# Attention stage on eight cores: the row-sum matmuls spread between the score and attention-times-V matmuls, and a fourth scratch buffer

## The chip, the cores and the metric

The kernel runs on the 8 cores of one Trainium2 chip. Each core takes one of the 8 batch items (x[c], 2048 tokens by 2048 features) with all the weights and writes its own part of the output; the cores exchange nothing. The metric is the device time of the slowest core in microseconds (us).

## The reference, cut to what matters

One transformer layer: layer norm, attention with 16 query heads and 4 key/value heads (head size 128), a feed-forward part, and the product of both on top of x.

```python
xn = _layernorm(x)
s = attn(xn)                      # below
g = silu(ffn(xn))                 # 2048 -> 5632 -> 2048
out = x + s * g
# attn, per head h, S = 2048:
q, k = rope(rms_norm(xn @ Wq.T)), rope(rms_norm(xn @ Wk.T)); v = xn @ Wv.T
bias = einsum('bhsr,bhtr->bhst', Rq, Rk)   # rank 32, heads 0..11; heads 0..3 made symmetric
scores = einsum('bhsd,bhtd->bhst', q, k) * scale + bias
attn = softmax(where(causal, scores, min), axis=-1)
out = einsum('bhst,bhtd->bhsd', attn, v) @ Wo.T
```

## The kernel before, in words

The program is a row of stages: p0 (layer norm and transposes), p1 (v, k and the rank-32 projections), p2 (q), p3 (feed-forward in two halves of the tokens), p4 (attention), p5 (the Wo projection), p6 (gating and output). The engines run their own instruction streams and meet at semaphores; within an engine the order is the order of the code. The change touches p4 alone.

p4 works in four blocks g = 0 to 3 (called blocks 1 to 4 here), each over 512 query tokens (a barrier stands between blocks). In block g each of the 16 heads h goes over nch = 4g + 4 chunks of 128 keys. Scores are kept with keys on the partitions and the 512 queries along the row.

- TensorE (from L1123). For chunk j: the score matmul (L1155, p_sc<-p_qg,p_kfm), for heads 0 to 11 a bias matmul (L1162) into the same bank, for heads 0 to 3 a second one (L1168). So a chunk costs three, two or one score matmuls in heads 0 to 3, 4 to 11 and 12 to 15. The score bank sc_ps has room for two pairs of chunks: a pair waits (eEv) until VectorE has emptied the pair two before it. From chunk 6 on, after the scores of chunk j comes the attention-times-V matmul ("AV") of chunk j - 6 (L1179), and after the loop the last six AVs (L1186). Each waits (eEx) for the exponentials of its pair. Then come the nch row-sum matmuls (L1194, p_sm<-p_ptb,c_onesc: a column of ones times the exponentials, into one row sm_ps), after a wait (eSv) for sm_ps to be empty; the last one signals eAV. Then bcast (L1134) of head h - 1: a matmul that copies the reciprocal of its sums to all partitions (rb_ps). Before a head from h = 2 on starts, TensorE waits (eNo) until VectorE has finished tail(h - 2).
- VectorE. For head h: sums_evac(h - 1) (L1208, empties sm_ps, signals eSv), then each pair of chunks from sc_ps to the scratch scr, as one copy of 128x1024 (L1241) or, in the last four chunks, as two additions of the causal mask (L1253, 128x512); then tail(h - 1): rb_ps to rb_sb (L1218) and the normalised output to ogs (L1222), which waits (eB2) for bcast(h - 1). Here sums_evac and tail of a head come one head late. A pair takes scratch buffer pr % 3, and waits (eEx) until ScalarE has read what was in it.
- ScalarE. Per pair the exponential of the scratch into ptb (L1290, bf16), with a bound found before as the bias; after a head's pairs recip_chain(h - 1) (L1275 and L1278: logarithm, then exponential of the negative), which signals eSm, for which bcast waits.
- SyncE loads the q of 8 heads at a time (L1105, L1114; the second load waits for head 7's last sum matmul) and stores ogs.

```python
if h >= 1:
    tensor.wait_ge(eSv.h, base_eSv + h)
for jj in range(nch):
    mm2 = tensor.matmul(sm_ps[0:1, 0:512], onesc[:, :], ptb[:, jj * 512:(jj + 1) * 512],
                        start=(jj == 0), stop=(jj == nch - 1))
mm2.then_inc(eAV.h, 1)
if h >= 1:
    bcast(tensor, h - 1)
```

Of the kernel before, what the change touches and what calls it, by code (L numbers as in the profile page):

```python
# [9 lines left out]
F32 = mybir.dt.float32  # L10
# [37 lines left out]
def build_program(taps=(), stop_after=None):  # L48
# [53 lines left out]
    with ExitStack() as L0:  # L102
# [5 lines left out]
        onesc = sbuf("c_onesc", [128, 1], BF16)  # L108
# [47 lines left out]
        with ExitStack() as SA:  # L156
# [5 lines left out]
            with ExitStack() as SP:  # L162
                sb = lambda n, sh, dt: SP.enter_context(nc.sbuf_tensor(n, sh, dt))
# [775 lines left out]
        if go("p4"):  # L939
            with ExitStack() as SP:  # L940
# [146 lines left out]
                eQl = sem("eQl"); eSp4 = [sem(f"eSp{i}") for i in range(4)]  # L1087
                scr = sb("p4_scr", [128, 3 * 1024], F32)
                for g in range(NG):
                    nch = 4 * g + 4  # L1090
                    with nc.Block(f"p4g{g}") as block:
# [39 lines left out]
                        def _(tensor):  # L1131
# [10 lines left out]
                            for h in range(NH):  # L1142
# [7 lines left out]
                                for j in range(nch):  # L1150
# [25 lines left out]
                                    if j >= 6:  # L1176
# [5 lines left out]
                                            ptb[:, jj * 512:(jj + 1) * 512],  # L1182
                                            start=(jj == 0), stop=False)
                                for jj in range(max(0, nch - 6), nch):
                                    tensor.wait_ge(eEx.h, base_eEx + pbase + jj // 2 + 1)
# [4 lines left out]
                                        start=(jj == 0), stop=(jj == nch - 1))  # L1190
                                if h >= 1:
                                    tensor.wait_ge(eSv.h, base_eSv + h)
                                for jj in range(nch):
                                    mm2 = tensor.matmul(  # L1194
                                        sm_ps[0:1, 0:512],
                                        onesc[:, :], ptb[:, jj * 512:(jj + 1) * 512],
                                        start=(jj == 0), stop=(jj == nch - 1))
                                mm2.then_inc(eAV.h, 1)
# [6 lines left out]
                        def _(vector):  # L1205
# [24 lines left out]
                            for h in range(NH):  # L1230
                                if h >= 1:
                                    sums_evac(vector, h - 1)
                                for j in range(0, nch, 2):
                                    pr = ich // 2
                                    if pr >= 3:
                                        vector.wait_ge(eEx.h, base_eEx + pr - 2)
                                    po = (pr % 2) * 1024
                                    so = (pr % 3) * 1024
                                    if j + 1 < 4 * g:
# [29 lines left out]
                        def _(scalar):  # L1269
# [14 lines left out]
                            for h in range(NH):  # L1284
                                for p in range(nch // 2):
# [5 lines left out]
                                        ptb[:, j0 * 512:(j0 + 2) * 512],  # L1291
                                        scr[:, (pr % 3) * 1024:(pr % 3) * 1024 + 1024],
                                        AF.Exp,
# [248 lines left out]
```

## Time and profile before

| what | value |
|---|---|
| time, median of 3 runs | 4578.66 us (lowest 4578.41) |
| profiled execution: its own time | 4576.78 us |
| its span on core 7, the slowest | 4575.2 us (the eight cores: 4552.0 to 4575.2) |
| mean granted TensorE clock of the core | 0.901 of full speed |
| TensorE matmul busy | 3566.5 us, 78% of the span |
| VectorE, ScalarE busy | 1117.7 us (24%), 906.3 us (20%) |
| p4, four blocks | 3108.6 to 4166.6 us of the span |

The profile is of one execution on the slowest core. A table of stretches gives the busy time of each engine in a window, with the number of instructions, and the clock that TensorE was granted, as a share of full speed (2.4 GHz; the other level is 1.2 GHz). The timeline lists instructions with their start, duration, engine, line, output and inputs; "xN" stands for N alike in a row, and what is in brackets is how long the engine sat idle before it and what ended that. A matmul of 512 columns is listed with 0.38 us from its start to its end at the full clock, but the next one can start earlier; the distance between starts is what it costs in a stream.

### The profile page before, as it was taken

The page shows a single profiled execution, that of the slowest core. Times are in us where ns is not written, and L with a number is a line of the kernel's source. Part 1 is how long each engine was busy: PE and PEld are TensorE (multiplying, and loading weights), DVE is VectorE, ACT ScalarE, POOL GpSimd, SP SyncE. Part 2 cuts the span into 40 slices and gives each one's busy share as a digit, 9 for nine tenths or more (in the row PEclk, how much of TensorE's full clock was granted, in tenths as well). Part 3 has the DMA queues.
Part 4 walks back from the last instruction along what each step waited for, and adds up shares of the span by engine and source line. Part 5 has one row for each costly group of instructions (what it writes and reads, how often), then busy time and mean ns, then how long its engine had stood idle before and what let it go on. Part 6 is the DMA issues. An engine that isn't in the chain of part 4 may idle for free. (4 is left out here: it accounts for less than half of the span.)

```text
span 4575.2 us, 38843 instructions; the slowest of 8 cores (4552.0 to 4575.2 us)
## 1 busy us (share of the span) xinstructions
PE 3566.5 (78%) x15274; PEld 1498.9 (33%) x15274; DVE 1117.7 (24%) x1179; ACT 906.3 (20%) x895; POOL 390.9 (9%) x343
## 2 busy tenths in 40 slices
PE   2576477776999998998999999764677877785973
PEld 1222122222444443443444444321122222222433
DVE  7132133342001000000000000023444554552006
ACT  2121033331000000001000000002333444452112
POOL 0000011111111110001111110000000000000000
PEclk9977788888999999999999999987787988997986
DMA  3311412214777864547777855441000000003347
GB/s 130 62 12 19 109 30 37 35 30 51 79 74 75 80 67 73 75 74 82 76 74 78 79 60 78 78 115 45 20 19 19 7 18 15 15 6 92 38 115 276
DMA packets 547235, 287.85 MB, mean 63 GB/s; under 512 B 457075, under 2 KB 528756, under 8 KB 540020
## 3 DMA queue, kind: packets, MB, share of 16 engines
q0 software_dynamic: 498480, 162.55, 33.2%
q1 hardware_dynamic: 48580, 122.82, 7.8%
q8 instruction: 128, 2.10, 0.2%
q14 instruction: 47, 0.39, 0.0%
HBM read 397.53 MB, written 50.33 MB: 98 GB/s over the span
## 5 line engine op out<-in xcount | busy, mean ns | idle before, releaser
L900 PE MATMUL p_dps<-p_hfm,p_dwb 128*128 128x512 bf16 x2816 | 625.6, 385 | 86.2 <-ACT p_gout L918 59.6
L828 PE MATMUL p_gps<-xn_fm,p_gwb 128*128 128x512 bf16 x2816 | 626.6, 381 | 39.1 <-DMA p_uwb<-wu 39.1
L835 PE MATMUL p_ups<-xn_fm,p_uwb 128*128 128x512 bf16 x2816 | 622.1, 379 | 0.0
L861 DVE SCALAR_TENSOR_TENSOR p_hfm<-p_ups,c_ups,p_sg 128x1024 bf16<-128x1024 f32 x88 | 113.0, 1284 | 1499.8 <-ACT p_sg L850 1499.8
L1290 ACT ACTIVATE p_ptb<-p_scr,st_bnegb 128x1024 bf16<-128x1024 f32 x320 | 366.2, 1148 | 524.5 <-DVE p_scr L1241 408.9
L1155 PE MATMUL p_sc<-p_qg,p_kfm 128*128 128x512 bf16 x640 | 280.9, 456 | 193.1 <-DVE p_ogs L1222 97.6
L900 PEld LDWEIGHTS p_dps<-p_hfm,p_dwb 128*128 128x128 bf16 x2816 | 277.4, 99 | 434.3 <-issue 116.5
L828 PEld LDWEIGHTS p_gps<-xn_fm,p_gwb 128*128 128x128 bf16 x2816 | 276.5, 98 | 375.6 <-issue 46.5
L835 PEld LDWEIGHTS p_ups<-xn_fm,p_uwb 128*128 128x128 bf16 x2816 | 275.5, 98 | 332.3
L697 PE MATMUL p_qps<-xn_fm,p_wbuf 128*128 128x512 bf16 x1024 | 287.0, 438 | 37.6 <-DMA p_wbuf<-wq 37.6
L850 ACT ACTIVATE p_sg<-p_gps,c_gates 128x1024 f32<-128x1024 f32 x88 | 98.1, 1115 | 1089.7 <-PE p_ups L835 1089.6
L1241 DVE COPY p_scr<-p_sc 128x1024 f32<-128x1024 f32 x192 | 232.3, 1223 | 135.6 <-PE p_sc L1162 61.8
L1342 PE MATMUL p_sps<-p_osb,p_wob 128*128 128x512 bf16 x1024 | 223.9, 382 | 39.4 <-DMA p_wob<-wo 39.4
L1162 PE MATMUL p_sc<-p_rqs,p_rku 128*128 128x512 bf16 x480 | 208.8, 435 | 0.0
L1155 PEld LDWEIGHTS p_sc<-p_qg,p_kfm 128*128 128x128 bf16 x640 | 67.0, 108 | 385.1 <-issue 355.1
L810 POOL DMA_DIRECT2D p_gwb<-wg x88 | 100.7, 1144 | 1016.6 <-PE p_ups L835 990.2
L697 PEld LDWEIGHTS p_qps<-xn_fm,p_wbuf 128*128 128x128 bf16 x1024 | 106.5, 109 | 221.0 <-issue 141.2
L1186 PE MATMUL p_o<-p_ptb,p_vsb 128*128 128x512 bf16 x352 | 110.5, 402 | 79.5 <-ACT p_ptb L1290 78.9
L1253 DVE TENSOR_TENSOR p_scr<-p_sc,p_masks 128x512 f32<-128x512 f32 x256 | 163.3, 684 | 32.6 <-PE p_sc L1168 18.3
L1342 PEld LDWEIGHTS p_sps<-p_osb,p_wob 128*128 128x128 bf16 x1024 | 100.8, 99 | 163.6 <-issue 44.5
L1194 PE MATMUL p_sm<-p_ptb,c_onesc 128*1 128x512 bf16 x640 | 153.5, 388 | 0.0
L918 ACT ACTIVATE p_gout<-p_dps,c_downs 128x1024 bf16<-128x1024 f32 x32 | 34.1, 1111 | 512.6 <-PE p_dps L900 478.8
(138 smaller groups left out, 2486.4 us busy)
## 6 DMA issues: line engine op xcount, KB each, us to landing
p_gwb<-wg POOLq DMA_DIRECT2D x88, 512.0 KB, 6.3
p_uwb<-wu POOLq DMA_DIRECT2D x88, 512.0 KB, 8.1
p_dwb<-wd POOLq DMA_DIRECT2D x88, 512.0 KB, 5.7
p_xt<-x SPq DMA_DIRECT2D x32, 1024.0 KB, 8.1
y<-p_outb SPq DMA_DIRECT2D x16, 1024.0 KB, 11.0
p_wbuf<-wq POOLq DMA_DIRECT2D x16, 512.0 KB, 6.4
sp_q<-p_qout SPq DMA_DIRECT2D x64, 128.0 KB, 1.8
sp_g<-p_gout SPq DMA_DIRECT2D x32, 256.0 KB, 3.0
```

The costliest lines, as they stand in the source:

```text
L697: mm = tensor.matmul(qps[:, po + q4 * 512:po + (q4 + 1) * 512], wv_[:, ec * 128:(ec + 1) * 128], xn_cols(ec, hh * 1024 + q4 * 512, 512), s ...
L828: tensor.matmul(gps[:, po + q4 * 512:po + (q4 + 1) * 512], gw_[:, ec * 128:(ec + 1) * 128], xn_cols(ec, hh * 1024 + q4 * 512, 512), start= ...
L835: mm = tensor.matmul(ups[:, po + q4 * 512:po + (q4 + 1) * 512], uw_[:, ec * 128:(ec + 1) * 128], xn_cols(ec, hh * 1024 + q4 * 512, 512), s ...
L861: vector.scalar_tensor_tensor(hfm[:, ic * 1024:(ic + 1) * 1024], ups[:, po:po + 1024], ups_c[:, ic:ic + 1], sg[:, po:po + 1024], ALU.mult, ...
L900: mm = tensor.matmul(dps[:, oc4 * 1024 + q4 * 512: oc4 * 1024 + (q4 + 1) * 512], wv_[:, oc4 * 128:(oc4 + 1) * 128], hfm[:, ic * 1024 + q4 ...
L1155: last = tensor.matmul(sc_ps[:, po:po + 512], kfm[:, kv * S + j * 128: kv * S + (j + 1) * 128], qg[:, (h % 8) * 512:(h % 8 + 1) * 512], st ...
L1162: last = tensor.matmul(sc_ps[:, po:po + 512], rku[:, h * S + j * 128: h * S + (j + 1) * 128], rqs[:, oc * S + g * 512: oc * S + (g + 1) * ...
L1194: mm2 = tensor.matmul(sm_ps[0:1, 0:512], onesc[:, :], ptb[:, jj * 512:(jj + 1) * 512], start=(jj == 0), stop=(jj == nch - 1))
L1241: vector.tensor_copy(scr[:, so:so + 1024], sc_ps[:, po:po + 1024]).then_inc(eEv.h, 1)
L1253: op = vector.tensor_tensor(scr[:, soc:soc + 512], sc_ps[:, poc:poc + 512], masks[:, k * 512:(k + 1) * 512], ALU.add)
L1290: scalar.activation(ptb[:, j0 * 512:(j0 + 2) * 512], scr[:, (pr % 3) * 1024:(pr % 3) * 1024 + 1024], AF.Exp, bias=bneg_b[:, col:col + 1]). ...
L1342: mm = tensor.matmul(sps[:, po + q4 * 512:po + (q4 + 1) * 512], wv_[:, ec * 128:(ec + 1) * 128], osb[:, ec * S + q4 * 512: ec * S + (q4 + ...
```

## The change

The nch sum matmuls of a head are issued in groups of four, each behind the AV of the last chunk of its group (jj % 4 == 3), wherever that AV stands: in the loop over the chunks (new line 1188) or after it (new line 1203). The wait for eSv moves to the first group. The accumulation in sm_ps now lies between matmuls into o_ps and sc_ps, which are other banks. The scratch scr has four buffers of 1024 columns in place of three, and VectorE's wait for a free one goes back one pair further. No instruction of VectorE, ScalarE or SyncE moves.

```diff
-                scr = sb("p4_scr", [128, 3 * 1024], F32)
+                scr = sb("p4_scr", [128, 4 * 1024], F32)
...
                                             start=(jj == 0), stop=False)
+                                        if jj % 4 == 3:
+                                            if jj == 3 and h >= 1:
+                                                tensor.wait_ge(eSv.h, base_eSv + h)
+                                            for js in range(jj - 3, jj + 1):
+                                                tensor.matmul(
+                                                    sm_ps[0:1, 0:512], onesc[:, :],
+                                                    ptb[:, js * 512:(js + 1) * 512],
+                                                    start=(js == 0), stop=False)
                                 for jj in range(max(0, nch - 6), nch):
                                     tensor.wait_ge(eEx.h, base_eEx + pbase + jj // 2 + 1)
...
-                                if h >= 1:
-                                    tensor.wait_ge(eSv.h, base_eSv + h)
-                                for jj in range(nch):
-                                    mm2 = tensor.matmul(
-                                        sm_ps[0:1, 0:512],
-                                        onesc[:, :], ptb[:, jj * 512:(jj + 1) * 512],
-                                        start=(jj == 0), stop=(jj == nch - 1))
+                                    if jj % 4 == 3:
+                                        if jj == 3 and h >= 1:
+                                            tensor.wait_ge(eSv.h, base_eSv + h)
+                                        for js in range(jj - 3, jj + 1):
+                                            mm2 = tensor.matmul(
+                                                sm_ps[0:1, 0:512], onesc[:, :],
+                                                ptb[:, js * 512:(js + 1) * 512],
+                                                start=(js == 0), stop=(js == nch - 1))
...
-                                    if pr >= 3:
-                                        vector.wait_ge(eEx.h, base_eEx + pr - 2)
+                                    if pr >= 4:
+                                        vector.wait_ge(eEx.h, base_eEx + pr - 3)
                                     po = (pr % 2) * 1024
-                                    so = (pr % 3) * 1024
+                                    so = (pr % 4) * 1024
...
-                                        scr[:, (pr % 3) * 1024:(pr % 3) * 1024 + 1024],
+                                        scr[:, (pr % 4) * 1024:(pr % 4) * 1024 + 1024],
```

On TensorE, the end of a head with two score matmuls a chunk in block 4 (16 chunks), before. p_sc are scores, p_o is AV, p_sm are the sums, p_rb is the broadcast:

```order
L1155 MATMUL p_sc<-p_qg,p_kfm 128x512
L1162 MATMUL p_sc<-p_rqs,p_rku 128x512
L1179 MATMUL p_o<-p_ptb,p_vsb 128x512
L1186 MATMUL p_o<-p_ptb,p_vsb 128x512 x6
L1194 MATMUL p_sm<-p_ptb,c_onesc 1x512 x16
L1134 MATMUL p_rb<-p_recip,c_onesr 128x512
```

The same place after the change, from the AV of chunk 7 on:

```order
L1179 MATMUL p_o<-p_ptb,p_vsb 128x512
L1188 MATMUL p_sm<-p_ptb,c_onesc 1x512 x4
L1155 MATMUL p_sc<-p_qg,p_kfm 128x512
L1162 MATMUL p_sc<-p_rqs,p_rku 128x512
L1179 MATMUL p_o<-p_ptb,p_vsb 128x512
L1155 MATMUL p_sc<-p_qg,p_kfm 128x512
L1162 MATMUL p_sc<-p_rqs,p_rku 128x512
L1179 MATMUL p_o<-p_ptb,p_vsb 128x512
L1194 MATMUL p_o<-p_ptb,p_vsb 128x512 x2
L1203 MATMUL p_sm<-p_ptb,c_onesc 1x512 x4
L1194 MATMUL p_o<-p_ptb,p_vsb 128x512 x4
L1203 MATMUL p_sm<-p_ptb,c_onesc 1x512 x4
L1134 MATMUL p_rb<-p_recip,c_onesr 128x512
```

Of the 16 sums that stood together ahead of the broadcast, four are left there; four stand between the AVs after the loop, and eight in the loop (four of them shown, four more behind AV 3). In block 2 (8 chunks), TensorE at the end of such a head, before:

```order
L1155 MATMUL p_sc<-p_qg,p_kfm 128x512
L1162 MATMUL p_sc<-p_rqs,p_rku 128x512
L1179 MATMUL p_o<-p_ptb,p_vsb 128x512
L1186 MATMUL p_o<-p_ptb,p_vsb 128x512 x6
L1194 MATMUL p_sm<-p_ptb,c_onesc 1x512 x8
L1134 MATMUL p_rb<-p_recip,c_onesr 128x512
```

And after:

```order
L1155 MATMUL p_sc<-p_qg,p_kfm 128x512
L1162 MATMUL p_sc<-p_rqs,p_rku 128x512
L1179 MATMUL p_o<-p_ptb,p_vsb 128x512
L1194 MATMUL p_o<-p_ptb,p_vsb 128x512 x2
L1203 MATMUL p_sm<-p_ptb,c_onesc 1x512 x4
L1194 MATMUL p_o<-p_ptb,p_vsb 128x512 x4
L1203 MATMUL p_sm<-p_ptb,c_onesc 1x512 x4
L1134 MATMUL p_rb<-p_recip,c_onesr 128x512
```

Here no sum stands ahead of a score matmul of the same head.

## Rows read from the trace of the kernel before

**Rows 1.** Stretches, p4's blocks: us, busy PE PEld DVE ACT POOL, PEclk, DMA.

```profile
3108.60:3289.80 181.20, 108.68 (x288) 30.87 (x288) 74.05 (x112) 56.37 (x65) 0.00 (x0) 0.75 0.07 24
3289.80:3521.80 232.00, 163.81 (x544) 52.99 (x544) 108.93 (x144) 93.00 (x97) 0.00 (x0) 0.84 0.06 19
3521.80:3813.40 291.60, 217.39 (x800) 75.58 (x800) 148.12 (x176) 129.57 (x129) 0.00 (x0) 0.89 0.05 15
3813.40:4166.60 353.20, 278.38 (x1056) 99.26 (x1056) 186.81 (x208) 166.25 (x161) 0.00 (x0) 0.90 0.04 13
```

**Rows 2.** Waits in 3100 to 4170: us in total, times, longest.

```profile
PE p_sc L1155 <- DVE p_ogs L1222: 97.6, 52, 2.2
PE p_o L1186 <- ACT p_ptb L1290: 78.9, 117, 2.1
...
PE p_sc L1155 <- DVE p_scr L1241: 23.5, 50, 1.0
...
DVE p_scr L1241 <- ACT p_ptb L1290: 1.3, 1, 1.3
```

**Rows 3.** Timeline, TensorE, end of head 11 in block 4.

```profile
4067.92 0.38 PE L1179 MATMUL p_o<-p_ptb,p_vsb 128*128 128x512 bf16 x1
4068.26 0.38 PE L1155 MATMUL p_sc<-p_qg,p_kfm 128*128 128x512 bf16 x1
...
4069.12 0.38 PE L1162 MATMUL p_sc<-p_rqs,p_rku 128*128 128x512 bf16 x1
...
4069.55 0.59 PE L1186 MATMUL p_o<-p_ptb,p_vsb 128*128 128x512 bf16 x2
4070.70 0.59 PE L1186 MATMUL p_o<-p_ptb,p_vsb 128*128 128x512 bf16 x2 [0.55 <-ACT p_ptb L1290]
4071.89 0.59 PE L1186 MATMUL p_o<-p_ptb,p_vsb 128*128 128x512 bf16 x2 [0.60 <-ACT p_ptb L1290]
4072.42 3.61 PE L1194 MATMUL p_sm<-p_ptb,c_onesc 128*1 128x512 bf16 x16
4075.96 1.12 PE L1134 MATMUL p_rb<-p_recip,c_onesr 1*128 1x512 f32 x2
4079.00 1.86 PE L1155 MATMUL p_sc<-p_qg,p_kfm 128*128 128x512 bf16 x4 [1.92 <-DVE p_ogs L1222]
```

**Rows 4.** Timeline, ScalarE, the same head.

```profile
4068.21 3.54 ACT L1290 ACTIVATE p_ptb<-p_scr,st_bnegb 128x1024 bf16<-128x1024 f32 x3 [0.27 <-DVE p_scr L1241]
...
4072.34 0.63 ACT L1278 ACTIVATE p_recip<-p_recip 1x512 f32<-1x512 f32 x1
```

**Rows 5.** Timeline, TensorE, end of head 0 in block 4 (last score matmul, last AVs).

```profile
3833.21 0.38 PE L1168 MATMUL p_sc<-p_rksh,p_rqu 128*128 128x512 bf16 x1
...
3835.77 0.59 PE L1186 MATMUL p_o<-p_ptb,p_vsb 128*128 128x512 bf16 x2 [1.11 <-ACT p_ptb L1290]
```

**Rows 6.** Timeline, TensorE, end of head 13 in block 4.

```profile
4107.61 0.38 PE L1179 MATMUL p_o<-p_ptb,p_vsb 128*128 128x512 bf16 x1
4108.10 0.38 PE L1155 MATMUL p_sc<-p_qg,p_kfm 128*128 128x512 bf16 x1
...
4108.53 0.38 PE L1155 MATMUL p_sc<-p_qg,p_kfm 128*128 128x512 bf16 x1
...
4111.73 0.59 PE L1186 MATMUL p_o<-p_ptb,p_vsb 128*128 128x512 bf16 x2 [0.60 <-ACT p_ptb L1290]
```

**Rows 7.** Timeline, TensorE, last AVs of head 15 in block 2.

```profile
3508.79 0.59 PE L1186 MATMUL p_o<-p_ptb,p_vsb 128*128 128x512 bf16 x2 [0.33 <-ACT p_ptb L1290]
```

**Rows 8.** Timeline, TensorE, end of head 6 in block 1.

```profile
3179.15 1.02 PE L1194 MATMUL p_sm<-p_ptb,c_onesc 128*1 128x512 bf16 x4
3180.10 1.12 PE L1134 MATMUL p_rb<-p_recip,c_onesr 1*128 1x512 f32 x2
```

**Rows 9.** Stretches: behind a head's end in block 4, and 40 us of the feed-forward stage.

```profile
4119.40:4125.40 6.00, 5.26 (x13) 1.51 (x12) 4.80 (x4) 3.68 (x4) 0.00 (x0) 0.50 0.07 24
...
2420.00:2460.00 40.00, 40.00 (x187) 18.18 (x186) 3.85 (x3) 3.35 (x3) 6.85 (x6) 1.00 0.74 73
```

## The prediction

> **What bounds the kernel now.** I read the table of stretches first, one row for each of the four query blocks of the attention stage [rows 1]. The stage is 1058 us of 4575.2, and TensorE is the busiest engine in every block: in the last 278.4 us of 353.2, against 186.8 for VectorE and 166.2 for ScalarE. So the stage ends when TensorE has done its matmuls, and what can be won without taking matmuls away is TensorE's idle time (72.5, 68.2, 74.2 and 74.8 us in the four blocks) and the time in which its clock is low. The waits say what the idle time is made of [rows 2]: 97.6 us before the first score matmul of a head, until VectorE has normalised the head before the last (p_ogs); 78.9 us before an attention-times-V matmul ("AV" below), until ScalarE's exponentials (p_ptb) are there; 23.5 us before a score matmul, until VectorE has emptied the score bank. Then I went through one head in order of time.
>
> Rows 3 are the end of a head with two score matmuls per chunk, in the fourth block. Matmuls of one stream start 0.216 us apart. The last score matmul starts at 4069.12, the AV of chunk 9 follows, then AV 10 and 11; AV 12 and 13 wait for ScalarE (0.55 idle), AV 14 and 15 again (0.60). Only then come the 16 row-sum matmuls, 3.61 us, then the broadcast of the previous head's reciprocal at 4075.96, then 1.92 us idle until VectorE is done, and at 4079.00 the next head's scores. During the sums VectorE and ScalarE have nothing to do. What ends this chain is the last exponential, not TensorE's own work: TensorE stands idle twice while it holds matmuls that could run. ScalarE ends the head's exponentials just before 4071.75 (4068.21 + 3.54) and the reciprocal at 4072.97 [rows 4].
>
> **The change, part by part.** It removes no matmul and adds none. (a) The sums of chunks 0 to 3 go behind AV 3, and so on by fours. A block of 4 chunks has the old order. With 8 chunks both groups of sums lie behind the last score matmul: the first moves ahead of AV 4. With 12 chunks one group moves in between score matmuls and one between AV 7 and AV 8. With 16 chunks two groups move in between score matmuls and one between AV 11 and AV 12. Four sums always stay at the end. One group is 4 x 0.216 = 0.86 us. (b) The wait for the emptied sum bank comes earlier in the head. VectorE empties that bank ahead of the head's first score copy, several us before AV 3, so I cost the wait at nothing. (c) VectorE's scratch gets a fourth buffer. VectorE waited 1.3 us in all for a free one [rows 2]: nothing, and at most 1.3.
>
> What (a) gives is TensorE's idle time that the moved sums fill. I take G, the time from the end of the last score matmul's slot to the start of the last AV pair. In G lie five AVs (1.08 us) and idle time. Nothing can make G shorter than VectorE's last masking, the last exponential and the semaphores between them.
>
> Heads 0 to 3 (three score matmuls a chunk): TensorE sets the pace in the loop, so its row shows the shortest G [rows 5]: 3835.77 - 3833.42 = 2.35 us (the slot of the last score matmul, from 3833.21, ends at 3833.42), 1.27 of it idle. One group of sums fits, 0.41 stays idle. A group placed among the score matmuls only delays them, and comes back as shorter work at the end. Gain 0.86 in each of the three blocks: 12 heads x 0.86 = 10.3 us.
>
> Heads 4 to 11 (two score matmuls): G = 4071.89 - 4069.34 = 2.55 us [rows 3], 1.47 idle. The group in G gives 0.86. In blocks 3 and 4 the groups in the loop delay the last score matmul, and G may then shrink to 2.35: another 0.20. They also fill the small holes that TensorE has in the loop: from 4067.92 to 4068.26 is 0.34 instead of 0.216, a hole of 0.13, and there are two such behind the first group in block 4 (0.26), while in block 3 I take 0.05. Block 2: 0.86, block 3: 1.11, block 4: 1.32. Eight heads each: 26.3 us.
>
> Heads 12 to 15 (one score matmul): VectorE sets the pace. G = 4111.73 - 4108.74 = 2.99 us, and the hole from 4107.61 to 4108.10 is 0.27 [rows 6]. Block 4: 0.86 + (2.99 - 2.35) + 2 x 0.27 = 2.04. Block 3: one group in the loop costs 0.86 - 0.27 = 0.59, which G takes up whole, so the whole 1.73 us of two groups would be won; one of its four heads has less idle time, so I take 1.6. Block 2: the gain is the idle before the last AVs; it differs between the four heads, the last one has 0.33 us listed [rows 7], which is some 0.5 between the slots; I take 0.5. Four heads each: 4 x (0.5 + 1.6 + 2.04) = 16.6 us.
>
> Sum: 10.3 + 26.3 + 16.6 = 53 us.
>
> What is late next? After the change the last sum ends 0.86 us after AV 15, about 1.4 us after the last exponential, and the broadcast behind it needs ScalarE's reciprocal, which ends 1.3 us after the exponential [rows 4]. That is close, but block 1 already has just this order, and there the broadcast follows the four sums at once (sums from 3179.15, broadcast at 3180.10, no idle) [rows 8]. So it costs nothing. The wait for p_ogs (1.92) stays as it is, since VectorE's two operations follow the broadcast. The block ends and the two loads of Q in each block stay too.
>
> Bounds of this term. If a group in the loop delays VectorE by its whole length and fills no hole, each head wins only the group in G: 44 x 0.86 + 4 x 0.5 = 40 us. If every moved sum were free, the gain would be (4 + 8 + 12) x 16 x 0.216 = 83 us. I take 53, since rows 3, 5 and 6 are nearest to it.
>
> The unknown is the clock. The granted clock is 0.75, 0.84, 0.89 and 0.90 in the four blocks [rows 1], which is a mixture of the two levels, 1.2 and 2.4 GHz: low for 50%, 32%, 22% and 20% of the time. In blocks 2 to 4 that is 74 + 64 + 71 = 209 us at the low level, of which TensorE is busy about three quarters (659.6 of 876.8 us), and half of that is lost: 78 us. It falls after the idle time at a head's end: the stretch of 6 us behind such an end is at 0.50, and dense work just before this stage was at 1.00 [rows 9]. The change makes the idle time before the last AV shorter and leaves the 1.9 us; it also brings the two nearer to each other. I see no sign for one direction and take nothing, with 20 us either way.
>
> The Trainium skill, TensorE: Matmul & The Clock Gate, section "A second HAM failure mode: psum-queue depth-cycling", says that a kernel whose TensorE idles briefly and often between groups of matmuls sees its clock go to and fro. This trace agrees: 0.84 to 0.90 in blocks with three or four short waits a head, against 1.00 in the dense stretch. By that rule fewer waits mean more clock, which is rival B below.
> The same page, in its section "Seeing it yourself", warns of a limiter that lowers the clock of a die to 13/16 once three of its cores run dense matmuls. That would speak against filling TensorE's holes. This trace does not show it: 1.00 in the dense stretch, with all eight cores at the same work.
>
> The profiled execution took 4576.8 us (span 4575.2), the median of the runs shown is 1.9 us above. So 4576.8 - 53 = 4523.8 by the profile and 4525.6 against the median: I say 4525.
>
> **The rivals.** (A) The sums in the loop delay VectorE fully. For it: VectorE's copies run nearly back to back in the loop, and TensorE is never more than two pairs ahead of it; against it: the holes of 0.13 and 0.27 us. Gain 40, time 4539.
>
> (B) The clock rises as the waits go. If half of the low time in blocks 2 to 4 went away, 39 us more: 4486. For it: the clock is higher the less of a block TensorE idles (0.75 at 40% idle, 0.90 at 21%) [rows 1]; against it: the 1.9 us wait, after which it falls, is left in every head.
>
> (C) The clock falls, and the change is slower than before. Place: the end of a head in blocks 2 to 4. The dense run of 8 to 16 sums ahead of the 1.9 us idle becomes 4 sums, which is the shape of block 1, and block 1 has 0.75. At 0.75 the work of blocks 2 to 4, 877 - 53 - 78 = 746 us, would stretch by the low half: T = 746 + 0.5 x T x 0.75 / 2, T = 918, against 824: 94 us more, 4576.8 - 53 + 94 = 4618. It decides from the point where the loss by the low clock reaches 78 + 53 = 131 us: 349 us at the low level, 40% of the blocks, a mean clock of 0.80. Against it: block 1's heads are 10 us with the same idle time as the heads of 20 us in block 4, so it has twice as much of it per us.
>
> (D) The change does not do what it says: the filled holes come back before the broadcast or at the p_ogs wait, since ScalarE's reciprocal is only 0.1 us ahead. Then 4577. Against it: rows 8.
>
> **How the numbers follow.** Forecast 0.70, A 0.13, B 0.08, C 0.06, D 0.03. Range: at the fast end all moved sums free (4577 + 2 - 83 = 4496), or B in part; at the slow end A with 15 us lost by the clock: 4554. I give 4492 to 4555; B's far end, C and D lie outside. A change of over 2% (92 us, about what a measurement of this kernel can tell from no change) needs a time under 4487 or over 4670. Faster by that much: 0.06, most of B. Slower by that much: 0.02, the far end of C, since C itself is only 0.9% slower. Within 2%: 0.92.
>
> **What would show each step.** Right: TensorE's busy time in the stage and the count of sum matmuls as before; TensorE's wait for p_ptb down from 78.9 us to about 40 (block 1's 27 stay, and some 0.3 a head elsewhere); the wait for p_ogs still near 98 us; VectorE's wait for the broadcast shorter by 0.9, 1.7 and 2.6 us a head in blocks 2, 3 and 4, less what the loop gives back; block 1 unchanged in length, block 2 about 12, block 3 about 19, block 4 about 22 us shorter; in blocks 2 to 4 a granted clock within 0.02 of now. Wrong: a new wait of the broadcast for p_recip in each head (D); VectorE waiting longer for p_sc in the loop and the last exponential late by the whole 0.86 or 1.73 us (A); a mean clock of blocks 2 to 4 above 0.93 (B) or under 0.80 (C).

## The result, and the profile after

The changed kernel takes 4548.6 us in the median of 23 runs, the kernel before 4583.5 us in the same series. The ratio is 0.9921, with a 95% interval of 0.9903 to 0.9939: some 36 us (28 to 44) faster, or 0.8%, where 53 us were forecast. Some executions of every kernel take longer, with a lower granted clock on the cores of one die: the ratios leave them out, and one profile below is therefore read on six cores. "Block lengths" are means over the eight cores of the profiled executions, from one block's first load of Q to the next block's. A mean of eight cores moves by about 1 us between profiles of the same order of work.

| kernel | block 1 | block 2 | block 3 | block 4 | stage | ratio to before (95%) |
|---|---|---|---|---|---|---|
| before | 182.5 | 232.8 | 292.0 | 354.4 | 1061.7 | |
| after | 182.7 | 222.8 | 277.6 | 339.4 | 1022.4 | 0.9921 (0.9903 to 0.9939) |
| forecast for after | as before | -12 | -19 | -22 | -53 | |

The stretches of the four blocks after, on the slowest core, to lay beside [rows 1] (columns as there):

```profile
3107.40:3289.00 181.60, 110.34 (x288) 30.82 (x288) 74.08 (x112) 56.60 (x65) 0.00 (x0) 0.75 0.07 24
3289.00:3513.00 224.00, 170.71 (x544) 52.04 (x544) 109.60 (x144) 93.18 (x97) 0.00 (x0) 0.80 0.06 19
3513.00:3790.30 277.30, 222.79 (x800) 71.44 (x800) 149.65 (x176) 130.12 (x129) 0.00 (x0) 0.88 0.05 16
3790.30:4127.80 337.50, 283.25 (x1056) 93.61 (x1056) 188.48 (x208) 166.94 (x161) 0.00 (x0) 0.89 0.04 13
```

The reader is to see two things. The count of matmuls in each block is the same, and block 1 is unchanged. But TensorE's busy time has grown in blocks 2 to 4: 163.8, 217.4 and 278.4 us before, 170.7, 222.8 and 283.3 now. In means of eight cores the stage went from 771.4 us busy and 290.3 idle to 784.8 busy and 237.7 idle. So 52.7 us of listed idle time went, and 13.4 us came back as longer work for the same matmuls.

That 52.7 is so near the 53 of the forecast is partly luck. A matmul is listed 0.16 us longer than its slot of 0.216, so each wait that goes takes less listed idle time with it than it is worth; and by the account below the changed order fills 9 us of idle time more than the forecast counted. The two work against each other.

The waits of the stage after, beside [rows 2]:

```profile
PE p_sc L1155 <- DVE p_ogs L1231: 97.3, 52, 2.2
...
PE p_o L1194 <- ACT p_ptb L1299: 28.3, 43, 1.7
...
PE p_sc L1155 <- DVE p_scr L1250: 19.3, 38, 1.4
...
PE p_rb L1134 <- ACT p_recip L1287: 15.1, 4, 3.8
```

The wait for the exponentials fell from 78.9 to 28.3 us, of which 25.5 are block 1's: blocks 2 to 4 have 2.8 us left. The wait for p_ogs stays at 97 us. The broadcast waits for the reciprocal four times, at the blocks' ends, as before. Where the longer work is, the end of head 10 in block 4 shows, in order of time on TensorE, to lay beside [rows 3]:

```profile
4019.19 0.38 PE L1179 MATMUL p_o<-p_ptb,p_vsb 128*128 128x512 bf16 x1
4019.50 1.02 PE L1188 MATMUL p_sm<-p_ptb,c_onesc 128*1 128x512 bf16 x4
4020.46 0.39 PE L1155 MATMUL p_sc<-p_qg,p_kfm 128*128 128x512 bf16 x1
4020.68 0.38 PE L1162 MATMUL p_sc<-p_rqs,p_rku 128*128 128x512 bf16 x1
...
4021.33 0.38 PE L1162 MATMUL p_sc<-p_rqs,p_rku 128*128 128x512 bf16 x1
4021.55 0.38 PE L1179 MATMUL p_o<-p_ptb,p_vsb 128*128 128x512 bf16 x1
4021.76 0.59 PE L1194 MATMUL p_o<-p_ptb,p_vsb 128*128 128x512 bf16 x2
4022.29 1.02 PE L1203 MATMUL p_sm<-p_ptb,c_onesc 128*1 128x512 bf16 x4
4023.24 1.25 PE L1194 MATMUL p_o<-p_ptb,p_vsb 128*128 128x512 bf16 x4
4024.42 1.02 PE L1203 MATMUL p_sm<-p_ptb,c_onesc 128*1 128x512 bf16 x4
4025.37 1.12 PE L1134 MATMUL p_rb<-p_recip,c_onesr 1*128 1x512 f32 x2
4028.38 0.38 PE L1155 MATMUL p_sc<-p_qg,p_kfm 128*128 128x512 bf16 x1 [1.89 <-DVE p_ogs L1231]
```

Starts within one kind of matmul are 0.216 us apart. From the AV to the first sum it is 0.31 (4019.19 to 4019.50), and from the first sum to the score matmul behind the four 0.96 (to 4020.46) in place of 0.86. So a run of sums costs 0.19 us beyond its matmuls, 0.09 at its start and 0.10 at its end, and the profile counts it as busy, not as idle. The weight loads in the same place show where it arises (columns as before, PEld is the loading of the stationary operand):

```profile
4018.98 0.10 PEld L1179 LDWEIGHTS p_o<-p_ptb,p_vsb 128*128 128x128 bf16 x1
4019.50 0.52 PEld L1188 LDWEIGHTS p_sm<-p_ptb,c_onesc 128*1 128x1 bf16 x4 [0.42 <-issue]
4020.45 0.10 PEld L1155 LDWEIGHTS p_sc<-p_qg,p_kfm 128*128 128x128 bf16 x1 [0.44 <-issue]
4020.47 0.10 PEld L1162 LDWEIGHTS p_sc<-p_rqs,p_rku 128*128 128x128 bf16 x1
```

The load for the AV at 4019.19 begins at 4018.98, a whole matmul ahead. The load of the 128x1 column for the sum at 4019.50 begins at 4019.50, and the next 128x128 load at 4020.45, for the matmul at 4020.46. Between a 128-column and a 1-column load nothing is loaded ahead. Load and matmul are listed with the same start, some 0.09 us after the slot of the AV ends (4019.19 + 0.216 = 4019.41); what fills these 0.09 us the profile does not say.
The Trainium skill, TensorE: Matmul & The Clock Gate, section "Step-by-step: what each phase is for", says that TensorE pulls a weight load ahead of the matmuls in flight, when their row groups don't conflict or the load goes to the background weight buffer. The trace agrees between 128-column loads (0.21 us ahead) and shows none ahead at a change to or from the 1-column one; whether one of the page's two conditions fails there no run shows.

The kernel before had 64 runs of sums in the stage, the changed one has 160. That these changes of width are what was lost was the theory for the experiments. Its rivals: the sums in the loop hold VectorE up (the prediction's rival A); the clock (in block 2 its mean over the eight cores fell from 0.837 to 0.815).

### The profile page after: what moved, and what is told of

The parts are those of the page before. It is cut to its first block and busy times, and to the rows that moved or that the text cites. A ratio compares the mean times of both kernels' runs of the same rounds, so it can differ in the third digit from the quotient of the medians.

```text
span 4537.9 us, 38839 instructions; the slowest of 8 cores (4518.4 to 4537.9 us)
## 1 busy us (share of the span) xinstructions
PE 3592.5 (79%) x15274; PEld 1494.8 (33%) x15274; DVE 1121.5 (25%) x1179; ACT 908.5 (20%) x895; POOL 391.0 (9%) x343
## 5 line engine op out<-in xcount | busy, mean ns | idle before, releaser
L828 PE MATMUL p_gps<-xn_fm,p_gwb 128*128 128x512 bf16 x2816 | 626.1, 381 | 42.6 <-DMA p_uwb<-wu 42.6
L1155 PE MATMUL p_sc<-p_qg,p_kfm 128*128 128x512 bf16 x640 | 288.0, 467 | 186.5 <-DVE p_ogs L1231 97.3
L1351 PE MATMUL p_sps<-p_osb,p_wob 128*128 128x512 bf16 x1024 | 222.8, 381 | 38.6 <-DMA p_wob<-wo 38.6
L1162 PE MATMUL p_sc<-p_rqs,p_rku 128*128 128x512 bf16 x480 | 217.9, 454 | 0.0
L1194 PE MATMUL p_o<-p_ptb,p_vsb 128*128 128x512 bf16 x352 | 111.2, 401 | 29.9 <-ACT p_ptb L1299 28.3
L1333 POOL DMA_DIRECT2D p_wob<-wo x16 | 18.3, 1143 | 1308.5 <-DVEq L1319 1095.6
```

What stands on the lines that cost most here:

```text
L828: tensor.matmul(gps[:, po + q4 * 512:po + (q4 + 1) * 512], gw_[:, ec * 128:(ec + 1) * 128], xn_cols(ec, hh * 1024 + q4 * 512, 512), start= ...
L1155: last = tensor.matmul(sc_ps[:, po:po + 512], kfm[:, kv * S + j * 128: kv * S + (j + 1) * 128], qg[:, (h % 8) * 512:(h % 8 + 1) * 512], st ...
L1162: last = tensor.matmul(sc_ps[:, po:po + 512], rku[:, h * S + j * 128: h * S + (j + 1) * 128], rqs[:, oc * S + g * 512: oc * S + (g + 1) * ...
L1194: tensor.matmul(o_ps[:, (h % 2) * 512:(h % 2) * 512 + 512], vsb[:, jj * 512 + kv * 128: jj * 512 + (kv + 1) * 128], ptb[:, jj * 512:(jj + ...
L1351: mm = tensor.matmul(sps[:, po + q4 * 512:po + (q4 + 1) * 512], wv_[:, ec * 128:(ec + 1) * 128], osb[:, ec * S + q4 * 512: ec * S + (q4 + ...
```

## The experiments

**The scratch buffer alone, and the order alone.**

```diff
-                scr = sb("p4_scr", [128, 3 * 1024], F32)
+                scr = sb("p4_scr", [128, 4 * 1024], F32)
```

> The kernel before with nothing but the fourth scratch buffer and the wait that goes with it; the sums stay in one run at a head's end. Theory (the buffer does nothing, since VectorE waited 1.3 us in all for one): ratio to the kernel before 1.000, the four attention blocks within 1 us of 182.5, 232.8, 292.0 and 354.4 us (mean of the eight cores). Rival (VectorE gets ahead and the last exponential comes sooner): block 4 shorter by 3 us or more.

Ratio 1.0004 (0.9985 to 1.0023); blocks 183.1, 231.9, 291.8 and 354.8 us.

> The changed kernel with the scratch back at three buffers: the order of the sums alone. Theory: the same as the changed kernel, ratio to the kernel before 0.992, blocks 182.7, 222.8, 277.6 and 339.4 us. Rival (with sums in the loop VectorE needs the fourth buffer to catch up): blocks 3 and 4 longer than the changed kernel's by 3 us or more.

Blocks 183.5, 223.4, 277.8 and 339.1 us, stage 1023.9 against 1022.4 (this one has a profile but no ratio). The fourth buffer does nothing, before or after: all that was gained is in the order of the sums.

**All sums but four behind the loop.** The group in the loop is taken out, and the condition behind it becomes:

```diff
-                                    if jj % 4 == 3:
+                                    if jj == nch - 1 or jj == nch - 5:
...
-                                        for js in range(jj - 3, jj + 1):
+                                        for js in range(0 if jj == nch - 5 else nch - 4, jj + 1):
```

> The changed kernel, but no sum goes between score matmuls: all sums but the last four stand in one run ahead of the last four AVs, in every block (in block 2 this is the order of the changed kernel). One run more per head than in the kernel before, instead of 1, 2 and 3. Theory 1 (each run of sums costs 0.19 us beyond its matmuls where TensorE has no idle time beside it, and sums in the loop only delay what comes after): the whole idle time before the last AV pair is filled, 1.27, 1.47 and 1.91 us in heads 0 to 3, 4 to 11 and 12 to 15, less 0.19 for the run: 21 us shorter than before in each of blocks 3 and 4, so block 3 271 us and block 4 333 us, block 2 as in the changed kernel (223); ratio to the kernel before 0.988 to 0.989, a little better than the changed kernel. Theory 2 (the holes in the loop are worth what the prediction took, and runs cost nothing extra): blocks 3 and 4 as in the changed kernel or longer, ratio 0.992 to 0.994.

Ratio 0.9893 (0.9874 to 0.9912); blocks 182.2, 223.5, 274.3 and 334.8 us. Block 3 is 3.3 and block 4 is 4.6 us shorter than in the changed kernel, as theory 1 wants and against theory 2, if less than the 6 us of the numbers given; its clock is a little lower in block 3 (0.863 against 0.879). The two ratios overlap, so the lead rests on one profile of each. Cores at the same clock show it more clearly: block 3 at 0.88 takes 272.3 us against 277.1 (4.9 less), block 4 at 0.89 takes 333.2 against 339.7 (6.5 less). So one run behind the loop is better than groups in the loop. How much of the lead is the runs' cost this experiment alone can't tell.

**Ones with 128 columns.** The same order as the changed kernel; the sums then stand in all 128 partitions.

```diff
+                onesw = sb("p4_onesw", [128, 128], BF16)
-                sm_ps = SP.enter_context(nc.psum_tensor("p4_sm", [1, 512], F32))
+                sm_ps = SP.enter_context(nc.psum_tensor("p4_sm", [128, 512], F32))
...
-                                                    sm_ps[0:1, 0:512], onesc[:, :],
+                                                    sm_ps[:, 0:512], onesw[:, :],
```

> The changed kernel with a 128x128 block of ones as the stationary operand of the sums in place of the 128x1 column; the sum matmuls write the same row into all 128 partitions, VectorE still reads one. Order and count of all matmuls unchanged. Theory 1 (the extra 0.19 us of a run of sums is the change between a 1-column and a 128-column weight load, which isn't loaded ahead): 64 last runs and 48 runs in the loop get cheaper by 0.19, 21 us in all: block 1 180, block 2 220, block 3 271.5, block 4 330 us, ratio to the kernel before about 0.987; from the last AV to the first sum 0.22 us in place of 0.31. Rival (the 0.19 us belongs to the change of PSUM bank or the accumulation of another group): no difference to the changed kernel, ratio 0.992, 0.31 us stays.

Ratio 0.9856 (0.9834 to 0.9878), stage 1000.5 us, 21.9 shorter than in the changed kernel; blocks 181.6, 220.1, 271.6 and 327.2, against 180, 220, 271.5 and 330 expected. TensorE in block 4, around a group in the loop:

```profile
3966.87 0.38 PE L1181 MATMUL p_o<-p_ptb,p_vsb 128*128 128x512 bf16 x1
3967.08 1.03 PE L1190 MATMUL p_sm<-p_ptb,p_onesw 128*128 128x512 bf16 x4
3967.95 0.38 PE L1157 MATMUL p_sc<-p_qg,p_kfm 128*128 128x512 bf16 x1
```

From AV to sum 0.21, from sum to score matmul 0.87: the 0.19 is gone, and the weight load for the sums begins one matmul ahead:

```profile
3966.65 0.10 PEld L1181 LDWEIGHTS p_o<-p_ptb,p_vsb 128*128 128x128 bf16 x1
3966.87 0.75 PEld L1190 LDWEIGHTS p_sm<-p_ptb,p_onesw 128*128 128x128 bf16 x4
```

The change of bank and of accumulation group is still there, and the order and number of the matmuls are the same, so the rival falls. Not all of the 21.9 us is the runs': block 4 also has a higher clock (0.910 against 0.891), which by the prediction's way of counting is (0.109 - 0.090) / 0.5 x 335 us x 0.83 / 2 = some 5 us (an estimate).

**The kernel before with the same ones.**

> The kernel before, sums still in one run at a head's end, with the 128x128 block of ones as stationary operand. Theory 1 (a run of 1-column sums costs 0.19 us extra where nothing hides it): one run per head, all on the path, 64 x 0.19 = 12 us, 3 us per block: 179.5, 230, 289 and 351.5 us; ratio to the kernel before 0.9974. Rival (the gain of the 128-column sums came through the interleaving or the clock alone): blocks as before within 1 us. Together with the run of the changed kernel with 128 columns it gives what the interleaving is worth without the cost of runs: 40 to 48 us.

Ratio 0.9995 (0.9982 to 1.0008); blocks 180.6, 233.3, 291.0 and 353.9 us (six cores), 2.9 us less in all. The expected 12 us were too many. TensorE at a head's end (core 7) shows the reason:

```profile
4057.32 0.59 PE L1188 MATMUL p_o<-p_ptb,p_vsb 128*128 128x512 bf16 x2 [0.60 <-ACT p_ptb L1292]
4057.75 3.61 PE L1196 MATMUL p_sm<-p_ptb,p_onesw 128*128 128x512 bf16 x16
4061.29 1.12 PE L1136 MATMUL p_rb<-p_recip,c_onesr 1*128 1x512 f32 x2
```

The run starts 0.43 us behind the AV pair, in place of 0.53 [rows 3]; but from its start to the broadcast it is 3.54 us as before: the change from the sums to the broadcast (one row, f32) costs the same with either width. Why was not tried. So only 0.10 a head could be won, 6.4 us; the ratio's interval (up to 8 us) allows that, the block lengths show 2.9.

Together with the run before it this one tests the forecast: the same change of order, with 128-column sums on both sides and so without the cost that a change of width brings.

| 128-column sums | block 1 | block 2 | block 3 | block 4 | stage |
|---|---|---|---|---|---|
| old order (six cores) | 180.6 | 233.3 | 291.0 | 353.9 | 1058.8 |
| order of the changed kernel | 181.6 | 220.1 | 271.6 | 327.2 | 1000.5 |
| difference | +1.0 | -13.2 | -19.4 | -26.7 | -58.3 |
| forecast | 0 | -12 | -19 | -22 | -53 |

The 40 to 48 us expected for it were too few. Block 3, with the same clock on both sides (0.88), is the cleanest: 19.4 us, where the forecast had 18.7 and its rival A 16 x 0.86 = 13.8. Block 4 has the higher clock in the new order (0.910 against 0.888), by the same way of counting worth some 6 of its 26.7 us.

**The order behind the loop with the same ones.**

> Sums of all but the last four chunks in one run ahead of the last four AVs, none in the loop, with the 128x128 block of ones. Theory 1: with the extra cost of a run gone, the holes in the loop are worth more than the idle time that four sums leave in G: the order of the changed kernel should be as good or better with 128 columns (block 4 327 us) than this one (330 us), while with 1 column this one was better by 4.6 us in block 4. Rival (sums in the loop cost for another reason, such as VectorE's pace): this one stays better by some 4 us: block 4 323 us.

Ratio 0.9873 (0.9827 to 0.9918), stage 996.9 us; block 3 267.7, block 4 327.4. By these means the order behind the loop loses its lead in block 4 (327.4 to 327.2) and keeps it in block 3 (267.7 to 271.6), and by the ratios the two orders are equal. But its clock in block 4 is lower (0.893 against 0.910). With sums in the loop all eight cores have 0.91 there, with sums behind it one has. Blocks 3 and 4, first on core 0 with sums in the loop, then on that one core (4) with sums behind it:

```profile
3499.07:3770.04 270.97, 210.54 (x784) 80.19 (x800) 149.55 (x176) 129.51 (x129) 0.00 (x0) 0.88 0.05 16
3770.04:4097.17 327.13, 266.26 (x1034) 105.16 (x1056) 188.35 (x208) 166.55 (x161) 0.00 (x0) 0.91 0.04 14
...
3506.56:3770.65 264.09, 209.28 (x800) 79.18 (x800) 148.22 (x176) 129.58 (x129) 0.00 (x0) 0.89 0.05 17
3770.65:4094.56 323.91, 267.68 (x1056) 103.63 (x1056) 186.87 (x208) 166.48 (x161) 0.00 (x0) 0.91 0.04 14
```

At equal clock the lead is 3.2 us in block 4, and 5.6 us in block 3 (two cores at 0.88 take 265.7 and 266.8, seven of the other kernel 271.8 in the mean). So theory 1's "as good or better" failed. That does not bring rival A back; the rows before the change account for the lead. Sums behind the loop can fill all the idle time before the last AV pair, 1.27, 1.47 and 1.91 us in the three kinds of head [rows 3], [rows 5], [rows 6]: some 24 us a block, where groups in the loop were forecast to give 18.7 and 22.2. That is a lead of 5 us in block 3 and 2 in block 4 with no cost of runs at all. With 1-column sums the loop order has one more costly run a head in block 4 than the other (3 us more: 5), in block 3 as many. Measured at equal clock in blocks 3 and 4: 5.6 and 3.2 us with 128 columns, 4.9 and 6.5 with one. These are estimates on few cores. In all four cases the order behind the loop had the lower clock; why is open.

**Groups of two.** More runs, in the changed kernel:

```diff
-                                    if jj % 4 == 3:
+                                    if jj % 2 == 1:
...
-                                        for js in range(jj - 3, jj + 1):
+                                        for js in range(jj - 1, jj + 1):
```

> The changed kernel (1-column sums) with groups of two sums in place of four: twice the number of runs. It leaves two sums behind the last AV in place of four, 0.43 us a head less (28 us in all), if ScalarE's reciprocal is there in time. Theory 1 (0.19 us per run where nothing hides it): in blocks 3 and 4 there are 3 and 5 runs in the loop in place of 1 and 2: 16 x 0.19 x (2 + 3) = 15 us longer, so of the 28 us only 13 are left; the reciprocal, which needs 1.3 us behind the last exponential, now comes later than the sums and takes most of that: equal to the changed kernel within 8 us, with a wait of the broadcast for p_recip in each head. Rival (runs cost nothing): 15 to 28 us shorter than the changed kernel, ratio 0.986 to 0.989.

Ratio 0.9955 (0.9935 to 0.9975): slower than the changed kernel, by 17 us in the stage. Blocks 175.6, 228.5, 286.8 and 348.4 us. Block 1, where TensorE still waits for the exponentials, wins 7.1 us by the shorter end (16 x 0.43 = 6.9). Block 2 loses 5.7, block 3 9.2, block 4 9.0. TensorE behind the loop, in block 3:

```profile
3704.51 0.59 PE L1188 MATMUL p_sm<-p_ptb,c_onesc 128*1 128x512 bf16 x2
3705.03 0.60 PE L1194 MATMUL p_o<-p_ptb,p_vsb 128*128 128x512 bf16 x2
3705.57 0.59 PE L1203 MATMUL p_sm<-p_ptb,c_onesc 128*1 128x512 bf16 x2
3706.09 0.60 PE L1194 MATMUL p_o<-p_ptb,p_vsb 128*128 128x512 bf16 x2
3706.63 0.59 PE L1203 MATMUL p_sm<-p_ptb,c_onesc 128*1 128x512 bf16 x2
```

A pair of sums and a pair of AVs should take 4 x 0.216 = 0.86 us; they take 1.06. TensorE has no idle time here any more, so that a shorter end wins nothing and each added run costs its 0.19: 16 heads x (2, 3 and 4 runs more) x 0.19 = 6.1, 9.1 and 12.2 us. Measured 5.7, 9.2 and 9.0. Sign and order of size fit the theory, but the sum is no proof of the dose: the clock of these blocks fell too (0.815 to 0.794, 0.879 to 0.863, 0.891 to 0.876), by the same way of counting some 4 us a block, and the cores at 0.88 in block 3 differ by 5.8 us (283.0 against 277.1). Of the shorter end at most the 0.22 us that were left between the last AVs can come back (4023.24 to 4024.42 is 1.18 us, four AVs and the change 0.96), 3.5 us a block. The direct measure is the 1.06 us above. The expectation's "equal within 8 us" and its wait for the reciprocal were wrong, because they took the end of the last exponential for the bound, and it was TensorE itself.

**Without the broadcast.** With the sums in all partitions the broadcast matmul and two copies by VectorE can go, and the wait before each head no longer holds TensorE up: ScalarE reads the sums from PSUM and writes the reciprocal for all partitions at the start of the next head, and VectorE normalises in that head's loop (two banks for the sums, by head).

```diff
+                                    if j == 2 and h >= 1:
+                                        tail(vector, h - 1)
...
-                                scalar.activation(recip[0:1, so:so + 512],
-                                                  sums_sb[0:1, so:so + 512], AF.Ln)
+                                scalar.activation(rb_sb[:, so:so + 512],
+                                                  smb[hb % 2][:, 0:512], AF.Ln)
...
-                                if h >= 1:
-                                    bcast(tensor, h - 1)
```

> The order of the changed kernel with 128-column sums, which leave the sum in all partitions: the broadcast matmul, VectorE's two copies of sums and reciprocal and their waits are gone; ScalarE takes the reciprocal of the 128 rows straight from PSUM at the start of the next head, VectorE normalises in that head's loop, two sum banks. Theory (after the change the largest idle time of TensorE, 1.9 us before each head, and the 1.1 us of the broadcast are what is left): 60 x 3.0 = 180 us shorter than the kernel with 128 columns, plus up to 50 us by the clock, whose falls follow that idle time: ratio to the kernel before 0.935 to 0.948, mean clock of the blocks over 0.93. Rival (ScalarE's two operations at the start of a head, 1.3 us, delay the exponentials and take the place of the wait): 100 us or less, ratio 0.964 or more.

Ratio 0.9421 (0.9387 to 0.9455). Stage 797.4 us, 203 less than with 128-column ones alone; blocks 132.4, 167.9, 221.1 and 276.1; mean clock 0.81, 0.94, 0.96 and 0.97. TensorE at a head's end in block 3:

```profile
3731.27 0.59 PE L1188 MATMUL p_o<-p_ptb,p_vsb 128*128 128x512 bf16 x2 [0.25 <-ACT p_ptb L1278]
3731.70 1.02 PE L1197 MATMUL p_sm<-p_ptb,p_onesw 128*128 128x512 bf16 x4
3732.56 0.38 PE L1149 MATMUL p_sc<-p_qg,p_kfm 128*128 128x512 bf16 x1
```

The next head's scores follow the sums at once. ScalarE's two operations delay nothing here: they end at 3734.12, and VectorE's first copy of scores ends at 3734.91. But not all of the old wait is won: TensorE's wait for the score bank rises from 22.0 us in 43 times to 59.8 in 88, and that for the exponentials from 42.6 to 55.2. A large part of the 203 us is the clock, by the prediction's way of counting some 66 us (0.74, 0.83, 0.88 and 0.91 before); the parts of this edit were not tried one by one.

**The same with all sums in one run at a head's end** (and three scratch buffers).

> The kernel without the broadcast matmul (128-column sums, reciprocal taken by ScalarE at the next head's start), but with all sums of a head in one run at its end and three scratch buffers, as in the kernel before. Theory (what the spread sums win is TensorE's wait for the last exponentials, 1.3 to 1.9 us a head in blocks 2 to 4, and has nothing to do with the broadcast): 40 to 60 us longer than the kernel without the broadcast and with spread sums, attention stage 840 to 860 us in place of 797, block 1 unchanged at 132 us, ratio to the kernel before 0.951 to 0.956. Rival (without the stall at a head's end the sums find cover anyway): within 10 us of it.

Ratio 0.9551 (0.9532 to 0.957), stage 853.4 us, 56 more than with spread sums; blocks 131.4, 181.0, 240.0 and 301.1. With 128-column sums the order was worth 58.3 us while the broadcast was there, so it is worth the same without it: TensorE's wait for the last exponentials is a loss of its own (92.9 us in 122 times here, 55.2 in 81 with spread sums), which nothing else covers.

**All 16 heads' q loaded at the block's start,** without the broadcast, and the two orders of sums.

```diff
-                qg = sb("p4_qg", [128, 8 * 512], BF16)
+                qg = sb("p4_qg", [128, 16 * 512], BF16)
```

> The kernel without the broadcast, sums spread, with room for the q of all 16 heads: both loads are issued at a block's start, so that TensorE doesn't wait 8.3 us in the middle of each block, nor start the ninth head at the low clock. Expected: 4 x 8.3 = 33 us shorter, up to 12 more by the clock, less some 2 us at each block's start where the two loads share the queues: attention stage 755 to 770 us, ratio to the kernel before 0.933 to 0.936. Rival (the two loads delay the first head by the length of a load, 5.5 us): 15 us shorter only.

Ratio 0.9367 (0.9349 to 0.9386), stage 769.9 us, 27.5 less: at the slow end of the expected 755 to 770. The wait for q is 36.9 us in 4 waits, where it was 60.2 in 8: those in the middle of a block are gone, but the ones looked at were 5.8 us and not 8.3. Those at a block's start are as long as before (7.6 to 9.8 us, before 7.4 to 10.0).

> The same with the sums in one run ahead of the last four AVs in place of groups in the loop. Theory (TensorE is busy without a hole from one head to the next in either order, so that the place of the sums decides no more): within 5 us of the kernel with groups in the loop. Rival (groups in the loop hold VectorE up): 10 us shorter or more.

Ratio 0.9376 (0.9358 to 0.9395), stage 765.4 us: no difference that the runs can tell. They are the fastest two that I ran, 6.3% and 6.2% faster than the kernel before, and some 5.6% faster than the changed one (0.9367 / 0.9921).

## Why the prediction was right in kind, and where its sum was off

- What bounds, and the idle time that the step "what (a) gives" counted: right. It shows where a run of sums costs little extra, between the two orders with 128-column sums: 58.3 us in the stage with some 6 us of clock in block 4, and 19.4 us in block 3, where 18.7 were forecast.
- The scratch buffer and the earlier wait for the sum bank: nothing, right (1.0004 for the buffer alone).
- "What is late next": right. The broadcast follows the last four sums without a wait (4024.42, 4025.37), the wait for p_ogs is 97.3 us.
- The term that was mis-sized is "one group is 4 x 0.216 = 0.86 us". A run of four 1-column sums between 128-column matmuls costs 1.05. In G this costs nothing: of the 0.41 us that the prediction left idle there, 0.19 went to it, which fits the wait for the exponentials: 2.8 us in blocks 2 to 4 where about 13 were expected. In the loop there is no idle time to take it: 16 runs in block 3 and 32 in block 4, 48 x 0.19 = 9 us. With it the forecasts of 19 and 22 us become 16 and 16; measured 14.4 and 15.0.
- The clock, for which I took nothing "with 20 us either way": block 2 won 10.0 in place of 12. In the changed kernel, cores at 0.84 and at 0.80 in this block can be compared (core 4, then core 5):

```profile
3282.64:3503.27 220.63, 165.01 (x544) 50.95 (x544) 108.85 (x144) 92.92 (x97) 0.00 (x0) 0.84 0.06 20
...
3288.97:3512.96 223.99, 170.71 (x544) 52.04 (x544) 109.60 (x144) 93.18 (x97) 0.00 (x0) 0.80 0.06 19
```

  The same work takes 3.4 us more at 0.80, and five of the eight cores are there, where all were at 0.83 to 0.84 before. That would account for the 2 us. Why these cores went down and three stayed was not tried. In blocks 3 and 4 the mean clock moved by 0.005 at most.
- Sum: 53 - 9 for the runs in the loop - 2 for the clock = 42; measured 39.3 in the profiles and 36 (28 to 44) by the ratio. The 3 us between 42 and 39.3 are open.
- The rivals: A gave 40 us, nearer to the result than the forecast, but for the wrong reason. Its 13.8 us for block 3 stand against 19.4 with 128-column sums. One of its signs did come, in part: VectorE waits longer for scores, 54.3 us in place of 43.6 in block 3 and 76.9 in place of 50.8 in block 4 on the profiled cores, or 0.7 and 1.6 us a head. By A it would be the groups' whole length, 1.05 and 2.1 us with the change of weights; the forecast let the last exponential be late too, by 1.73 - 1.17 = 0.6 and 2.59 - 1.39 = 1.2 us, and with 0.19 a run that is 0.75 and 1.6. B and C fell: the mean clock of blocks 2 to 4 is 0.87 in place of 0.88, not above 0.93 or under 0.80. D fell. By the time of the changed kernel alone A cannot be told from the forecast.

## What to carry to other kernels

Before you count moved matmuls by their spacing in a run, look at the spacing where the kind of matmul changes: a stationary operand of another width can cost at each change, and the profile books it as busy time. When a gap filler goes where TensorE idles, such a cost is free; in a stretch without idle time each piece pays it, so use few pieces. And look at what stands between two parts (here a broadcast from one row, with two copies and a wait): a 128-column block of ones gives the sum in all partitions for the same matmul time, and what it let go of was worth five times the change (203 us to 39).

And compare blocks at the same granted clock before you call two orders equal: in block 4 a difference of 0.02 hid a lead of 3 us.

## What the runs showed of the hardware that I had not expected

- Between a 128x128 and a 128x1 stationary operand (bf16) the load is not made ahead: 0.09 us at the change to it and 0.10 at the change back, at the full clock; with 128x128 on both sides both are 0. The run of 16 sums to the f32 broadcast takes some 0.09 us more than its slots with either width.
- Sums with 1 and with 128 columns have the same spacing (16 sums and what follows them: 3.54 us with either).
- Without the broadcast and the 1.9 us of idle time at each head's end the granted clock of blocks 2 to 4 is 0.94 to 0.97, where the same order of sums with them had 0.83 to 0.91, so more of the time is at the 2.4 GHz level; block 1, whose heads are the shortest, goes from 0.74 to 0.81 only.
